# Post-norm decoder layer on one core: up and down units in one line through all visits, and pairs that join every four visits

## The chip, the core and the metric

One core of a Trainium2 chip. The metric is the device time of one execution in microseconds. TensorE is called PE, VectorE DVE, ScalarE ACT, GpSimd POOL, SyncE SP; SP issues all DMAs here. A unit is a piece of work named below.

## What is computed

x is 16 sequences of 128 tokens of 256 numbers, float32. Three residual blocks, each followed by a layer norm:

```python
x = layernorm(x + attention(x))            # 16 heads of 16, with biases, output product and bias
x = layernorm(x + recurrence(x, ctx_1024)) # per token and channel, along the tokens:
#   out = A + exp(u + k) * (v * B + max(t - 1, 0))
#   A = exp(-w) * A + (t != 0) * exp(k) * v ;  B = exp(w) * B + (t != 0) * exp(-k)
x = layernorm(x + ffn(x))                  # 8 experts, K = 128 of 128 tokens each:
#   G = softmax(x @ Wg.T); every token goes through every expert:
#   sum over e of G[e] * (gelu(x @ W1[e] + b1[e]) @ W2[e] + b2[e]),  W1[e] 256 x 1024
```

K is as large as the sequence, so the top-k picks every token.

## The kernel before

Sequences go two by two: 8 pairs of 256 tokens. A product of float32 numbers is made of three matmuls on parts (hi x hi, hi x lo, lo x hi), so each operand has a part hi, made on ACT by a copy, and a part lo, made on DVE by `low`, a subtraction (L830).

The FFN is cut into visits. A visit is one expert's turn, expert n % 8 in visit n, for the one or two pairs that are active; a pair joins at visit `JOIN[p]` and stays for 8. With joins (0, 5, 8, 13, 16, 21, 24, 29) there are 37 visits: 0 to 4 and 32 to 36 with one pair, 27 with two. A visit has 8 up units and 8 down units with two pairs, 4 and 4 with one. An up unit (`up`, L627) is 128 or 256 hidden columns: 6 matmuls of 512 columns, or 12 of 256, into one of two `up_ps` banks. ACT makes gelu (`hidden`, L761) into one of three slots of h_all, then the copy h_hi (`hidden_hi`, L754) into one of four; DVE makes h_lo (`hidden_lo`, L997). A down unit (`down`, L649) is 12 matmuls that add into `down_ps`, which holds the visit's output until `add_expert` (L1002) on DVE has added it, times the gate, to acc; the first down unit of the next visit waits for all of that (semaphore `added`, L653).

The order of units is written out by `items(n)` (L57): U0 U1 U2 D0 U3 D1 U4 ... U7 D5 D6 D7 within each visit. Every engine walks the same items, and each item also carries steps of the next pair's attention and recurrence: pair p has 64 steps laid over `LENGTH[p]` items from item `BEGIN[p]`. Per item the order on ACT is: h_hi of the unit before if that was an up unit (L809), gelu of this one (L811), the attention steps, splits. DVE has add_expert at item 0, h_lo, the steps, splits. The steps named in the prediction: maxima of the scores (8, 10, 24, 26), exp (12, 13, 28, 29), transposes of the probabilities and their copies pt_hi and pt_lo (14, 17, 30, 32), product with the values (16, 19, 31, 34), exps of the recurrence (44), scans and the mix (48 to 52), transposes back (54), transposes to x2t, which the pair's FFN needs (58), routing (60 to 62), gates (0 and 3 of the next pair's steps). Exp and gelu are in different ACT tables, so changing between them is an ACT_TABLE_LOAD; copies need none.

Weights: visits 0 to 7 load float32 pieces (`load_piece`), split them on ACT and DVE and write both parts to DRAM (`keep`); visits 8 to 31 read those parts back (`load_kept`); visits 32 on load and split again. There are 4 pieces for each of w1 and w2. The tables SPLIT and LOAD say at which item a piece is brought in, once the last unit that reads its slot is past. A finished pair is normalised (`finish`) and stored by SP at items 2 and 4 of the next visit.

Of the kernel before, what the change touches and what calls it, by code (L numbers as in the profile page):

```python
# [20 lines left out]
def decoder_layer(nc, x, ctx_in, wq, wk, wv, wo, cols, bv, bo, wg, w1, b1, w2, b2, out):  # L21
# [31 lines left out]
    def units(n):  # L53

        return FC if len(active(n)) == 2 else G

    def items(n):  # L57

        m = units(n)
        order = [("U", u) for u in range(LAG)]  # L60
        for u in range(LAG, m):
            order += [("D", u - LAG), ("U", u)]
        return order + [("D", u) for u in range(m - LAG, m)]

    def splits(n, k):

        table = SPLIT_TWO if len(active(n)) == 2 else SPLIT_ONE
        return [(n + d, i, q) for d, i, q in table.get(k, []) if n + d < VISITS and n + d not in KEPT]

    def loads(n, k):  # L70

        table = LOAD_TWO if len(active(n)) == 2 else LOAD_ONE
        return [(n + d, i, q) for d, i, q in table.get(k, []) if n + d in KEPT]

    FIRST_UNIT = list(itertools.accumulate((units(n) for n in range(VISITS)), initial=0))
    FIRST_ITEM = list(itertools.accumulate((len(items(n)) for n in range(VISITS)), initial=0))
# [11 lines left out]
    with ExitStack() as ctx:  # L88
# [122 lines left out]

        def sequence(n, i, q):

            return 2 * G * turn_of(n) + ORDER.index((i, q))

        def by_chunk(t):
            return t.rearrange("p (c n) -> p c n", c=C)
# [136 lines left out]
        def _(sp):  # L354
# [7 lines left out]
                sp.dma_start(ctx_sb[:], ctx_in[PAIR * p:PAIR * (p + 1)].rearrange("j s d -> s j d")).then_inc(ctx_loaded, 16)  # L362

            def load_piece(m):
                n, j = divmod(m, 2 * G)
                if n >= E:
                    n += len(KEPT)
                if n >= VISITS:
                    return
                i, q = ORDER[j]  # L370
                if m >= RAW:
                    before, was = divmod(m - RAW, 2 * G)
                    which, part = ORDER[was]
                    sp.wait_ge((w1_ready, w2_ready)[which], G * before + part + 1)
# [39 lines left out]
                load_piece(m)  # L414
            load_x(1)
            load_ctx(1)
            for m in range(2 * G - 1):
                load_piece(m + RAW)
            for m in range(2 * G - 1):
                keep(0, *ORDER[m])  # L420

            for n in range(VISITS):
                for k in range(len(items(n))):
# [12 lines left out]
                    if k == STORE_ITEM:  # L436
                        for p in range(NPAIR):
                            if n == JOIN[p] + E:
                                store(p)
            store(NPAIR - 1)  # L440
            sp.wait_ge(stored, 16 * NPAIR)

# [2 lines left out]
        def _(pe):  # L445
# [203 lines left out]
            def down(n, u):  # L649

                unit = FIRST_UNIT[n] + u
                if u == 0 and n > 0:
                    pe.wait_ge(added, EVACUATED[n])  # L653
                weights(n, 1, u * G // units(n))
                pe.wait_ge(h_ready, unit + 1)
                pairs = len(active(n))
                for k in range(2 // pairs):
                    c = u if pairs == 2 else 2 * u + k
                    for a in range(pairs):
                        for j in range(PAIR):  # L660
# [12 lines left out]
                if s in ROUTE_STEP:  # L673
                    route(0, ROUTE_STEP.index(s))
            for n in range(VISITS):
                for k, (kind, u) in enumerate(items(n)):
                    if kind == "U":
                        up(n, u)
                    else:
                        down(n, u)  # L680
                    if n == 0:
                        for part in FIRST_ROUTE.get(k, []):
                            route(0, part)
# [10 lines left out]
        def _(act):  # L694
# [108 lines left out]
                if s in ROUTE_STEP:  # L803
                    route(0, ROUTE_STEP.index(s))
            for n in range(VISITS):
                order = items(n)
                for k, (kind, u) in enumerate(order):
                    if k > 0 and order[k - 1][0] == "U":
                        hidden_hi(n, order[k - 1][1])  # L809
                    if kind == "U":  # L810
                        hidden(n, u)  # L811
                    if n == 0:
                        for part in FIRST_ROUTE.get(k, []):
                            route(0, part)
# [12 lines left out]
        def _(dve):  # L827
# [240 lines left out]
                if s in ROUTE_STEP:  # L1068
                    route(0, ROUTE_STEP.index(s))
            for n in range(VISITS):  # L1070
                order = items(n)
                left = [p for p in range(NPAIR) if n == JOIN[p] + E]
                for k, (kind, u) in enumerate(order):
# [4 lines left out]
                    if k > 0 and order[k - 1][0] == "U":  # L1078
                        hidden_lo(n, order[k - 1][1])
                    if n == 0:  # L1080
                        for part in FIRST_ROUTE.get(k, []):
                            route(0, part)
# [9 lines left out]
                    if k == NORM3_ITEM:  # L1092
                        for p in left:
                            finish(p, 1)
            add_expert(VISITS - 1)
# [5 lines left out]
        def _(pool):  # L1101
# [61 lines left out]
                for i, q in FIRST_SPLIT.get(s, []):  # L1163
                    split_lo(0, i, q)
            for n in range(VISITS):
                for k in range(len(items(n))):
                    if k == 0:
                        for p in range(NPAIR):
                            if n == JOIN[p] + E:
                                finish(p)  # L1170
# [25 lines left out]
ORDER = [(0, 0), (0, 1), (1, 0), (0, 2), (1, 1), (0, 3), (1, 2), (1, 3)]  # L1196
SPLIT_TWO = {1: [(0, 1, 3)], 3: [(1, 0, 0)], 6: [(1, 0, 1)], 8: [(1, 1, 0)], 10: [(1, 0, 2)], 12: [(1, 1, 1)],
             14: [(1, 0, 3)], 15: [(1, 1, 2)]}
LOAD_TWO = {0: [(0, 1, 3)], 2: [(1, 0, 0)], 5: [(1, 0, 1), (1, 1, 0)], 9: [(1, 0, 2), (1, 1, 1)], 13: [(1, 0, 3), (1, 1, 2)]}
LOAD_ONE = {0: [(0, 1, 3)], 1: [(1, 0, 0)], 2: [(1, 0, 1)], 3: [(1, 0, 2), (1, 1, 0)], 5: [(1, 0, 3), (1, 1, 1)], 6: [(1, 1, 2)]}  # L1200
SPLIT_ONE = {1: [(0, 1, 3)], 2: [(1, 0, 0)], 3: [(1, 0, 1)], 4: [(1, 1, 0)], 5: [(1, 0, 2)], 6: [(1, 1, 1), (1, 0, 3)],
             7: [(1, 1, 2)]}
# [39 lines left out]
```

## Time and profile before

| | before |
|---|---|
| median of 3 runs | 1026.37 us (1025.46 to 1026.95) |
| the profiled execution | 1025.53 us, its span 1023.8 |
| PE busy | 917.6 us, 90% |
| DVE busy | 602.8 us, 59% |
| ACT busy | 602.0 us, 59% |
| DMA | 170.33 MB, mean 166 GB/s |

The profile gives for each engine when it was busy, and for each idle time the instruction that ended it. Matmul ends are modelled, and consecutive matmuls overlap in the records, so the time of one is the distance of two starts. The granted clock is a share of 2.4 GHz; 0.5 is the lower level, 1.2 GHz.

### The profile page before, as it was taken

The numbers are of one execution on the slowest core, as the hardware profiler recorded it, in microseconds if no ns is written. First come the engines' busy times: TensorE is split into PE (matmuls) and PEld (weight loads), VectorE is DVE, ScalarE is ACT, GpSimd is POOL, SyncE is SP. The second block draws the span as 40 slices with busy tenths as digits, with TensorE's granted clock in tenths as the row PEclk, the third lists the DMA queues.
The fourth block names the chain that finished last, engine by engine and source line by source line (L and its number), as shares of the span: only waits on it lengthen the run. The fifth ranks groups of instructions, "written<-read, shape, count | busy, mean of one in ns | idle before, by whom it ended". The sixth has DMA issues, their size and how long they took to land.

```text
span 1023.8 us, 17885 instructions
## 1 busy us (share of the span) xinstructions
PE 917.6 (90%) x6672; PEld 824.0 (80%) x6672; DVE 602.8 (59%) x1254; ACT 602.0 (59%) x1017; POOL 84.2 (8%) x116
## 2 busy tenths in 40 slices
PE   4558697988799989999899989999899989999997
PEld 3457586778688879888788879888798888899997
DVE  6747667776565555565556645565556636333765
ACT  4437775666556655555556655555566645444685
POOL 3301001100020001100020001100011000000000
PEclk8667987999999999999999999999999999999999
DMA  6337879755554545454544455445454545565350
GB/s 208 102 126 258 278 251 316 255 198 179 172 168 142 157 140 173 128 173 135 160 150 150 139 167 156 150 149 158 134 167 128 164 141 158 175 195 155 118 171 11
DMA packets 143541, 170.33 MB, mean 166 GB/s; under 512 B 11080, under 2 KB 110688, under 8 KB 143456
## 3 DMA queue, kind: packets, MB, share of 16 engines
q1 hardware_dynamic: 143456, 169.19, 52.3%
q8 instruction: 54, 0.88, 0.4%
q14 instruction: 31, 0.25, 0.1%
HBM read 133.50 MB, written 35.65 MB: 165 GB/s over the span
## 4 chain that ended last, share of the span: by engine, by line
PE 72%; DVE 12%; ACT 11%; issue 3%; DMA 0%; POOL 0%; SPq 0%; POOLq 0%; ACTq 0%; DVEq 0%
PE up_ps L448 11%; PE up_ps L450 10%; PE up_ps L449 10%; PE down_ps L664 10%; PE down_ps L666 9%; PE down_ps L665 9%; ACT probs L717 2%; ACT L717 2%; DVE h_lo L830 2%; DVE pt_lo L905 2%; PE bank L487 2%; PE bank L448 2%; PE bank L470 1%; PE bank L450 1%; PE bank L449 1%
## 5 line engine op out<-in xcount | busy, mean ns | idle before, releaser
L768 ACT ACTIVATE h_all<-up_ps,b_all 128x512 f32<-128x512 f32 (+1 forms) x296 | 182.4, 631 | 344.3 <-PE up_ps L450 340.0
L664 PE MATMUL down_ps<-w_hi,h_hi 128*128 128x256 f32 x1024 | 300.6, 294 | 32.0 <-DVE h_lo L830 31.9
L665 PE MATMUL down_ps<-w_lo,h_hi 128*128 128x256 f32 x1024 | 292.3, 285 | 0.0
L666 PE MATMUL down_ps<-w_hi,h_lo 128*128 128x256 f32 x1024 | 292.3, 285 | 0.0
L830 DVE TENSOR_TENSOR h_lo<-h_all,h_hi 128x512 fp32r<-128x512 f32 x256 | 176.7, 692 | 191.8 <-ACT h_hi L759 190.7
L664 PEld LDWEIGHTS down_ps<-w_hi,h_hi 128*128 128x128 f32 x1024 | 198.0, 193 | 46.2 <-issue 32.4
L448 PE MATMUL up_ps<-x2t_hi,w_hi 128*128 128x512 f32 (+1 forms) x592 | 224.7, 380 | 0.9 <-DVE x2t_lo L830 0.9
L449 PE MATMUL up_ps<-x2t_lo,w_hi 128*128 128x512 f32 (+1 forms) x592 | 219.4, 371 | 0.0
L450 PE MATMUL up_ps<-x2t_hi,w_lo 128*128 128x512 f32 (+1 forms) x592 | 219.3, 370 | 0.0
L665 PEld LDWEIGHTS down_ps<-w_lo,h_hi 128*128 128x128 f32 x1024 | 198.6, 194 | 4.4
L666 PEld LDWEIGHTS down_ps<-w_hi,h_lo 128*128 128x128 f32 x1024 | 198.6, 194 | 0.0
L759 ACT ACTIVATE h_hi<-h_all 128x512 fp32r<-128x512 f32 x256 | 161.8, 632 | 5.2
L450 PEld LDWEIGHTS up_ps<-x2t_hi,w_lo 128*128 128x128 f32 x592 | 115.0, 194 | 19.0
L448 PEld LDWEIGHTS up_ps<-x2t_hi,w_hi 128*128 128x128 f32 x592 | 116.0, 196 | 13.3 <-DVE x2t_lo L830 1.3
L449 PEld LDWEIGHTS up_ps<-x2t_lo,w_hi 128*128 128x128 f32 x592 | 116.1, 196 | 10.6
L830 DVE TENSOR_TENSOR w_lo<-w_raw,w_hi 128x512 fp32r<-128x512 f32 x97 | 66.0, 701 | 37.4 <-ACT w_hi L781 37.4
L1105 POOL TENSOR_TENSOR var_eps<-moments,eps_row 128x2 f32<-128x2 f32 x24 | 10.1, 422 | 790.8 <-DVE moments L841 790.8
L781 ACT ACTIVATE w_hi<-w_raw 128x512 fp32r<-128x512 f32 x104 | 62.7, 629 | 1.1 <-issue 1.1
L1010 DVE SCALAR_TENSOR_TENSOR acc<-down_ps,gate,acc 128x256 f32<-128x256 f32 x112 | 47.0, 476 | 27.5 <-PE down_ps L666 27.5
L905 DVE TENSOR_TENSOR pt_lo<-bank,pt_hi 128x512 f16<-128x512 f32 x58 | 37.4, 686 | 32.1 <-ACT pt_hi L724 32.1
L890 DVE TENSOR_REDUCE neg_max<-bank 128x4 f32<-128x512 f32 x62 | 39.8, 684 | 20.4 <-PE bank L487 20.1
L717 ACT ACTIVATE probs<-probs 128x512 f32<-128x512 f32 x64 | 36.7, 620 | 8.7 <-DVE probs L897 8.5
(172 smaller groups left out, 1008.5 us busy)
## 6 DMA issues: line engine op xcount, KB each, us to landing
w_hi<-w_parts SPq DMA_DIRECT2D x192, 256.0 KB, 3.1
w_lo<-w_parts SPq DMA_DIRECT2D x192, 256.0 KB, 3.4
w_raw<-in_w_dram SPq DMA_DIRECT2D x104, 256.0 KB, 3.8
w_parts<-w_hi SPq DMA_DIRECT2D x64, 256.0 KB, 3.7
w_parts<-w_lo SPq DMA_DIRECT2D x64, 256.0 KB, 4.1
x_in<-in_x_dram SPq DMA_DIRECT2D x8, 256.0 KB, 3.8
ctx_sb<-in_ctx_dram SPq DMA_DIRECT2D x8, 256.0 KB, 4.3
out_dram<-acc SPq DMA_DIRECT2D x8, 256.0 KB, 2.4
```

Source lines behind the costliest of these rows:

```text
L448: nc.tensor.matmul(ps, hi, rhs_hi, start=first, stop=False)
L449: nc.tensor.matmul(ps, hi, rhs_lo, start=False, stop=False)
L450: return nc.tensor.matmul(ps, lo, rhs_hi, start=False, stop=last)
L664: nc.tensor.matmul(ps, hi, w2h[:, c, :], start=c == 0 and j == 0, stop=False, skip_group_check=True)
L665: nc.tensor.matmul(ps, hi, w2l[:, c, :], start=False, stop=False, skip_group_check=True)
L666: mm = nc.tensor.matmul(ps, lo, w2h[:, c, :], start=False, stop=c == FC - 1 and j == PAIR - 1, skip_group_check=True)
L717: nc.scalar.activation(probs[:, u % 2, i], probs[:, u % 2, i], ACT.Exp).then_inc(probs_ready, 1)
L759: nc.scalar.activation(h_hi[:, unit % HALF, :], h_all[:, unit % HALL, :], ACT.Copy).then_inc(h_hi_ready, 1)
L768: a = nc.scalar.activation(h_all[:, unit % HALL, k * wide:(k + 1) * wide], up_ps[unit % 2][:, k * wide:(k + 1) * wide], ACT.Gelu_apprx_tan ...
L781: nc.scalar.activation(piece((w1_hi, w2_hi)[i], i, q), raw(m, i), ACT.Copy)\
L830: return nc.vector.tensor_tensor(dst, src, hi.bitcast(F32), ALU.subtract)
L905: nc.vector.tensor_tensor(pt_lo[:, u % 2, i], by_head(turned(p, u)[i]), pt_hi[:, u % 2, i], ALU.subtract)\
```

## The change

One line of units runs through all visits: `plan()` lists all up units in order and puts a down unit behind the up unit that is three later (for the first down unit of a visit four later). A two-pair visit is then U0 D5' U1 D6' U2 D7' U3 U4 D0 D1 U5 D2 U6 D3 U7 D4, where ' is the visit before. A pair joins every four visits (0, 4, 8, ... 28), which makes 36 visits, 28 of them with two pairs. The second pair's steps are laid over the first 28 items, visits 0 to 3; the third's over visits 4 to 7; from visit 8 on the steps begin with a visit, as before. A down unit waits for each `down_ps` bank by itself. add_expert, finish and store follow the last down unit of a visit by 1, 3 and 5 items. The tables of splits and loads are written anew for the new line, and the order of the pieces follows them.

```diff
-    def items(n):
-        m = units(n)
-        order = [("U", u) for u in range(LAG)]
-        for u in range(LAG, m):
-            order += [("D", u - LAG), ("U", u)]
-        return order + [("D", u) for u in range(m - LAG, m)]
+    def plan():
+        ups = [(n, u) for n in range(VISITS) for u in range(units(n))]
+        lines, downs = [[] for _ in range(VISITS)], 0
+        for g, (n, u) in enumerate(ups):
+            lines[n].append(("U", n, u))
+            while downs + LAG + (ups[downs][1] == 0) <= g:
+                lines[n].append(("D",) + ups[downs])
+                downs += 1
+        return lines[:-1] + [lines[-1] + [("D",) + unit for unit in ups[downs:]]]
...
+    def up_before(i):
+        return [LINE[i - 1][1:]] if i > 0 and LINE[i - 1][0] == "U" else []
+
+    def ended(i):
+        return [(n, [p for p in range(NPAIR) if n == JOIN[p] + E - 1]) for n in range(VISITS - 1) if LAST_DOWN[n] == i]
...
             def down(n, u):
                 unit = FIRST_UNIT[n] + u
-                if u == 0 and n > 0:
-                    pe.wait_ge(added, EVACUATED[n])
...
                     for a in range(pairs):
+                        if c == 0 and n > 0 and a < len(active(n - 1)):
+                            pe.wait_ge(added, EVACUATED[n - 1] + PAIR * (a + 1))
...
-                for k, (kind, u) in enumerate(order):
-                    if k > 0 and order[k - 1][0] == "U":
-                        hidden_hi(n, order[k - 1][1])
+                for k, (kind, visit, u) in enumerate(ITEMS[n]):
+                    for unit in up_before(FIRST_ITEM[n] + k):
+                        hidden_hi(*unit)
                     if kind == "U":
-                        hidden(n, u)
+                        hidden(visit, u)
...
-                    if k == 0 and n > 0:
-                        add_expert(n - 1)
+                    for done, left in ended(FIRST_ITEM[n] + k - 1):
+                        add_expert(done)
                         for p in left:
                             finish(p, 0)
...
-JOIN = (0, 5, 8, 13, 16, 21, 24, 29)
-BEGIN = (None, 0, 40, 88, 152, 216, 280, 344, 408)
-LENGTH = (None, 40, 48, 64, 64, 64, 64, 64, 64)
+JOIN = (0, 4, 8, 12, 16, 20, 24, 28)
+BEGIN = (None, 0, 28, 93, 157, 221, 285, 349, 413)
+LENGTH = (None, 28, 64, 64, 64, 64, 64, 64, 64)
...
-NORM3_ITEM, STORE_ITEM = 2, 4
+NORM3_AFTER, STORE_AFTER = 3, 5
+FIRST_PIECES = [(0, 0, 0), (0, 0, 1), (0, 0, 2), (0, 0, 3), (0, 1, 0), (0, 1, 1), (0, 1, 2)]
+FREE_FIRST = {0: [(0, 1, 3)], 1: [(1, 0, 0)], 2: [(1, 0, 1)], 3: [(1, 0, 2)]}
...
+        [{1: [(1, 0, 0)], 2: [(0, 1, 2)], 3: [(1, 0, 1)], 5: [(1, 0, 2)], 6: [(0, 1, 3)]},
+         {2: [(0, 1, 2)], 3: [(1, 0, 0)], 6: [(0, 1, 3)], 7: [(1, 0, 1)], 10: [(1, 1, 0)], 11: [(1, 0, 2)], 14: [(1, 1, 1)],
+          15: [(1, 0, 3)]}]]
```

## Rows read from the trace of the kernel before

**Rows 1.** Stretches: busy us (x instructions) of PE, PEld, DVE, ACT, POOL; clock, DMA
```profile
64.20:179.90 115.70, 92.58 (x716) 88.42 (x717) 78.38 (x162) 82.34 (x151) 8.85 (x10) 0.84 0.75 246
179.90:284.60 104.70, 90.01 (x663) 78.98 (x662) 69.57 (x141) 66.94 (x111) 7.41 (x8) 0.98 0.61 202
518.40:634.80 116.40, 110.56 (x807) 97.91 (x806) 67.00 (x142) 67.56 (x108) 11.04 (x14) 1.00 0.49 152
959.40:1005.80 46.40, 46.36 (x386) 45.66 (x385) 35.23 (x64) 37.97 (x80) 1.24 (x2) 1.00 0.44 137
```

**Rows 2.** Waits of PE, 518.4 to 634.8: us in total, times, longest us
```profile
PE down_ps L664 <- DVE h_lo L830: 5.7, 4, 2.9
```

**Rows 3.** Waits of PE over the whole span
```profile
PE down_ps L664 <- DVE h_lo L830: 31.9, 23, 3.9
```

**Rows 4.** Timeline of PE: start, us, first matmul of an up, a down, an up unit
```profile
615.99 0.39 PE L448 MATMUL up_ps<-x2t_hi,w_hi 128*128 128x512 f32 x1
...
617.38 0.28 PE L664 MATMUL down_ps<-w_hi,h_hi 128*128 128x256 f32 x1
...
618.82 0.39 PE L448 MATMUL up_ps<-x2t_hi,w_hi 128*128 128x512 f32 x1
```

**Rows 5.** Timeline of PE: pair 0's first and last transposes, pair 1's last
```profile
3.88 1.09 PE L470 MATMUL bank<-ident,x_in 128*128 128x128 f32 x4 [3.88 <-DMA x_in<-in_x_dram]
...
62.13 1.11 PE L585 MATMUL bank<-ident,x 128*128 128x128 f32 x4 [3.27 <-DVE x L848]
...
174.26 0.66 PE L585 MATMUL bank<-ident,x 128*128 128x128 f32 x4 [0.27 <-DVE x L848]
```

**Rows 6.** Timeline of ACT at the end of visit 17
```profile
571.93 0.69 ACT L768 ACTIVATE h_all<-up_ps,b_all 128x512 f32<-128x512 f32 x1 [2.23 <-PE up_ps L450]
572.64 1.28 ACT L717 ACT_TABLE_LOAD   x1
573.93 1.16 ACT L717 ACTIVATE probs<-probs 128x512 f32<-128x512 f32 x2
...
576.55 1.06 ACT L724 ACTIVATE pt_hi<-bank 128x512 f16<-128x512 f32 x2
```

**Rows 7.** Timeline of PE: the first up unit behind that product with the values
```profile
578.71 0.48 PE L448 MATMUL up_ps<-x2t_hi,w_hi 128*128 128x512 f32 x1
```

**Rows 8.** Timeline of DVE at the end of visit 17
```profile
577.15 1.29 DVE L905 TENSOR_TENSOR pt_lo<-bank,pt_hi 128x512 f16<-128x512 f32 x2 [0.83 <-ACT pt_hi L724]
```

**Rows 9.** Timeline of DVE: step 24, in visit 17
```profile
565.34 1.29 DVE L890 TENSOR_REDUCE neg_max<-bank 128x4 f32<-128x512 f32 x2 [1.30 <-PE bank L487]
566.54 1.28 DVE L897 TENSOR_TENSOR probs<-bank,neg_max 128x512 f32<-128x512 f32 x2
```

**Rows 10.** Timeline of DVE: first and last of six small operations for the gates
```profile
516.31 0.17 DVE L980 TENSOR_REDUCE route_sum<-route_exps 128x2 f32<-128x16 f32 x1 [0.32 <-ACT route_exps L749]
...
517.21 0.17 DVE L830 TENSOR_TENSOR gate_all<-gate,gate_all 128x16 fp32r<-128x16 f32 x1
```

**Rows 11.** Timeline of ACT at the end of visit 18
```profile
601.45 0.69 ACT L768 ACTIVATE h_all<-up_ps,b_all 128x512 f32<-128x512 f32 x1 [1.91 <-PE up_ps L450]
...
605.60 0.66 ACT L759 ACTIVATE h_hi<-h_all 128x512 fp32r<-128x512 f32 x1
606.28 1.28 ACT L768 ACT_TABLE_LOAD   x1
```

**Rows 12.** Timeline of DVE at the start of visit 19
```profile
608.84 1.66 DVE L1010 SCALAR_TENSOR_TENSOR acc<-down_ps,gate,acc 128x256 f32<-128x256 f32 x4 [1.86 <-PE down_ps L666]
610.42 1.36 DVE L863 TENSOR_TENSOR_SCAN inc_b<-decay_row,inc_b 128x128 f32<-128x128 f32 x4
...
613.67 1.27 DVE L830 TENSOR_TENSOR h_lo<-h_all,h_hi 128x512 fp32r<-128x512 f32 x2
...
618.18 0.69 DVE L955 TENSOR_TENSOR exp_k<-exp_k,y1t 128x512 f32<-128x512 f32 x1
```

**Rows 13.** Timeline of PE: the transposes of the mix, visit 19
```profile
620.21 0.38 PE L577 MATMUL bank<-ident,exp_k 128*128 128x128 f32 x2
```

More of the change, by code:

```diff
@@ L55, in units, with table @@
         return FC if len(active(n)) == 2 else G
-    def items(n):
-        m = units(n)
-        order = [("U", u) for u in range(LAG)]
-        for u in range(LAG, m):
-            order += [("D", u - LAG), ("U", u)]
-        return order + [("D", u) for u in range(m - LAG, m)]
+    def plan():
[7 more added lines that the diff above has]
+        return lines[:-1] + [lines[-1] + [("D",) + unit for unit in ups[downs:]]]
+    ITEMS = plan()
+    LINE = [item for line in ITEMS for item in line]
+    LAST_DOWN = [max(i for i, (kind, m, _) in enumerate(LINE) if kind == "D" and m == n) for n in range(VISITS)]
+    def table(n):
+        if n == 0:
+            return FREE_FIRST
+        return FREE[len(active(n - 1)) - 1][len(active(n)) - 1]
     def splits(n, k):
-        table = SPLIT_TWO if len(active(n)) == 2 else SPLIT_ONE
-        return [(n + d, i, q) for d, i, q in table.get(k, []) if n + d < VISITS and n + d not in KEPT]
+        return [(n + d, i, q) for d, i, q in table(n).get(k, []) if n + d < VISITS and n + d not in KEPT]
     def loads(n, k):
-        table = LOAD_TWO if len(active(n)) == 2 else LOAD_ONE
-        return [(n + d, i, q) for d, i, q in table.get(k, []) if n + d in KEPT]
+        return [(n + d, i, q) for d, i, q in table(n).get(k, []) if n + d in KEPT]
+    def up_before(i):
+        return [LINE[i - 1][1:]] if i > 0 and LINE[i - 1][0] == "U" else []
+    def ended(i):
+        return [(n, [p for p in range(NPAIR) if n == JOIN[p] + E - 1]) for n in range(VISITS - 1) if LAST_DOWN[n] == i]
     FIRST_UNIT = list(itertools.accumulate((units(n) for n in range(VISITS)), initial=0))
-    FIRST_ITEM = list(itertools.accumulate((len(items(n)) for n in range(VISITS)), initial=0))
+    FIRST_ITEM = list(itertools.accumulate((len(line) for line in ITEMS), initial=0))
+    PIECES = FIRST_PIECES + [piece for n in range(VISITS) for k in range(len(ITEMS[n])) for piece in splits(n, k)]
     EVACUATED = list(itertools.accumulate((PAIR * len(active(n)) for n in range(VISITS)), initial=0))
@@ L212, in sequence @@
         def sequence(n, i, q):
-            return 2 * G * turn_of(n) + ORDER.index((i, q))
+            return PIECES.index((n, i, q))
         def by_chunk(t):
@@ L364, in load_piece @@
             def load_piece(m):
[L365 to L368, printed above, removed]
+                if m >= len(PIECES):
                     return
-                i, q = ORDER[j]
+                n, i, q = PIECES[m]
                 if m >= RAW:
-                    before, was = divmod(m - RAW, 2 * G)
-                    which, part = ORDER[was]
-                    sp.wait_ge((w1_ready, w2_ready)[which], G * before + part + 1)
+                    before, which, part = PIECES[m - RAW]
+                    sp.wait_ge((w1_ready, w2_ready)[which], G * turn_of(before) + part + 1)
                 if i == 0:
@@ L416, in _ @@
             load_ctx(1)
-            for m in range(2 * G - 1):
+            for m in range(len(FIRST_PIECES)):
                 load_piece(m + RAW)
-            for m in range(2 * G - 1):
-                keep(0, *ORDER[m])
+            for first_piece in FIRST_PIECES:
+                keep(*first_piece)
             for n in range(VISITS):
-                for k in range(len(items(n))):
+                for k in range(len(ITEMS[n])):
                     for visit, i, q in splits(n, k):
@@ L435, in _ @@
                             load_ctx(p + 1)
[L436 to L439, printed above, removed]
+                    for _, left in ended(FIRST_ITEM[n] + k - STORE_AFTER):
+                        for p in left:
+                            store(p)
             store(NPAIR - 1)
@@ L675, in _ @@
             for n in range(VISITS):
-                for k, (kind, u) in enumerate(items(n)):
+                for k, (kind, visit, u) in enumerate(ITEMS[n]):
                     if kind == "U":
-                        up(n, u)
+                        up(visit, u)
                     else:
[L680 to L683, printed above, removed]
+                        down(visit, u)
+                    for part in FIRST_ROUTE.get(FIRST_ITEM[n] + k, []):
+                        route(0, part)
                     for p, s in steps(FIRST_ITEM[n] + k):
@@ L805, in _ @@
             for n in range(VISITS):
-                order = items(n)
-                for k, (kind, u) in enumerate(order):
-                    if k > 0 and order[k - 1][0] == "U":
-                        hidden_hi(n, order[k - 1][1])
+                for k, (kind, visit, u) in enumerate(ITEMS[n]):
+                    for unit in up_before(FIRST_ITEM[n] + k):
+                        hidden_hi(*unit)
                     if kind == "U":
-                        hidden(n, u)
-                    if n == 0:
-                        for part in FIRST_ROUTE.get(k, []):
-                            route(0, part)
+                        hidden(visit, u)
+                    for part in FIRST_ROUTE.get(FIRST_ITEM[n] + k, []):
+                        route(0, part)
                     for p, s in steps(FIRST_ITEM[n] + k):
@@ L1070, in _ @@
             for n in range(VISITS):
-                order = items(n)
-                left = [p for p in range(NPAIR) if n == JOIN[p] + E]
-                for k, (kind, u) in enumerate(order):
-                    if k == 0 and n > 0:
-                        add_expert(n - 1)
+                for k in range(len(ITEMS[n])):
+                    for done, left in ended(FIRST_ITEM[n] + k - 1):
+                        add_expert(done)
                         for p in left:
                             finish(p, 0)
[L1078 to L1082, printed above, removed]
+                    for unit in up_before(FIRST_ITEM[n] + k):
+                        hidden_lo(*unit)
+                    for part in FIRST_ROUTE.get(FIRST_ITEM[n] + k, []):
+                        route(0, part)
                     for p, s in steps(FIRST_ITEM[n] + k):
@@ L1091, in _ @@
                         split_lo(visit, i, q)
-                    if k == NORM3_ITEM:
+                    for _, left in ended(FIRST_ITEM[n] + k - NORM3_AFTER):
                         for p in left:
@@ L1165, in _ @@
             for n in range(VISITS):
[L1166 to L1170, printed above, removed]
+                for k in range(len(ITEMS[n])):
+                    for _, left in ended(FIRST_ITEM[n] + k - 1):
+                        for p in left:
+                            finish(p)
                     for p, s in steps(FIRST_ITEM[n] + k):
```

8 lines of the change are left out of this document (1 added, 7 removed), and 3 rows, old and new, of the table FREE.

## The prediction

> **What bounds the kernel now.** Read the stretches first [rows 1]. From visit 8 to visit 27 the kernel repeats one pattern of four visits, in which the next pair's attention is fitted; one of its five turns stands there (518.4 to 634.8, 116.4 us). TensorE is busy 110.6 us of it, VectorE and ScalarE 67 to 68 us. So PE is the bound, and it loses 5.8 us a turn. Who ends that loss [rows 2]: down units that wait for h_lo, four waits, 5.7 us. Over the span the same wait is the largest kind, 31.9 us [rows 3]. Visits 0 to 4 are different (first line of [rows 1]): 115.7 us with PE busy 92.6 at a granted clock of 0.84 and DMA at 0.75; visits 5 to 7 take 104.7 us with 90.0 busy.
>
> PE's own work follows from its issue times [rows 4]: an up unit takes 1.39 us (615.99 to 617.38), a down unit 1.44 us (to 618.82). A visit with two pairs is 8 of each, 22.6 us; with one pair 4 units of each, twelve 256-column matmuls in each, so 4 x 2 x 1.44 = 11.5 us; the last stretch of [rows 1] has four such visits in 46.4, 11.6 each. Attention of one pair on PE is 110.6 - 4 x 22.6 = 20 us.
>
> **Part 1: 37 visits become 36.** Ten one-pair visits and 27 two-pair visits become 8 and 28: the same 64 visits by a pair. PE's columns are the same, and 2 x 11.6 - 22.6 = 0.6 us is all that this saves. One visit's splitting of weights goes (8 pieces on ScalarE and VectorE, 2 MB read), at the end where PE is busy 46.36 of 46.40 us: nothing. So the count of visits is worth under 1 us; the change lives by the waits.
>
> **Part 2: visits 0 to 3.** Until the start of visit 4 PE now has 16 up and 12 down units (28 x 1.44 = 40.5 us) and pair 1's attention (20 us). What ends the stretch is pair 1's chain, because visit 4 needs its x2t. Before, its last transposes for that are at 174.26, 110 us after 64.2, behind 36 of 40 items [rows 5]. The bounds: if each item costs the chain nothing, it stays at 110 us; if all of the items' share is on it, take pair 0, whose chain ran without FFN units from its first transposes at 3.9 us to the same point at 62.1 [rows 5]: 58 us, with the projections' loads and splits in it, for which I take off 5: 53. Then 36 items cost 110 - 53 = 57 us, 1.6 each, and the 25 items that are left cost 40: 93 us. With three more items and the routing matmuls visit 4 starts at 64.2 + 97 us. I take the 97: with VectorE 78 and ScalarE 82 of 115.7 us busy [rows 1], each step stands in a queue behind the units' and splits' work, so items count; the bound on the other side is 110. DMA moves 28 pieces x 768 KB = 22 MB, 227 GB/s over 97 us, under the 246 of that stretch before.
>
> **Part 3: visits 4 to 7.** Four two-pair visits (90.5), the four downs of visit 3 (5.8) less the three of visit 7 that come later (4.3), attention 20: 112. Idle before in visits 5 to 7: 14.7. Now attention has four visits, but the splits of this stretch are in the queues; 5.8 (a turn now) and 15 are the bounds; I take 11.5, nearer to the upper, for 8 splits a visit on both elementwise engines. Sum 123.5. Visits 0 to 7 therefore take 97 + 123.5 = 220.5 against 220.4 before. At the end the last four visits carry three more down units: 46.4 + 4.3 = 50.7 against 57.0 for five. Together -6.2 us; + 0.3 for the last visit, where the added wait stands behind one up unit only.
>
> **Part 4: the line, in each turn.** What goes: the last down unit of a visit no longer stands two downs behind its up unit. New order within a visit: U0 D5 U1 D6 U2 D7 U3 U4 D0 D1 U5 D2 U6 D3 U7 D4 (D5 to D7 of the visit before). All waits of [rows 2] are at these ends, so 5.7 us a turn go. What is late next, place by place, with attention's steps at their item numbers:
>
> (a) Softmax to values, second half (steps 28 to 31 at items 12 to 15). Before, item 12 is U7: ScalarE does gelu, table load, exps, the copy h_hi, exps, and pt_hi begins 4.62 us after the gelu did (571.93 to 576.55) [rows 6]; the values are done when the next up begins at 578.71, 6.78 after that gelu [rows 7], with only 0.2 waited for pt_lo. Now item 12 is U6 and U7 is item 14, just ahead of the copies pt_hi: a table load (1.28) and a gelu (0.69) stand between exp and pt_hi. pt_hi begins 2.0 to 2.1 us later, and nothing covers it: PE has D3, U7, the transposes and D4, about 5.1 us, and then waits to 8.2 for the first pt_lo, which now begins 0.6 after pt_hi and takes 0.65 [rows 8]. +2.1 us.
>
> (b) The same for the first half (steps 12 to 16): a further up unit stands before the values, so the loss is between 2.1 - 1.4 = 0.7 and 2.1; I take 1.0.
>
> (c) Scores (steps 8, 10 and 24, 26). Step 8 mod 16 is now at D0. ScalarE's copy h_hi of U4 needs the slot that D0 frees, and VectorE takes h_lo of U4 before the maxima: 0.85 + 0.75 = 1.6 us after D0 (0.63 and 0.69 are their own times), then neg_max and probs 2.5 [rows 9] = 4.1; PE reaches the next scores after 0.5 + 1.44 + 1.39 = 3.35. +0.75 twice, 1.5. Bounds 0 and 2.5 each.
>
> (d) Gates: exp of the logits (step 62, item 14) now comes behind U7's gelu: 0.2 + 0.7 + 1.28 + 0.2 + 1.1 of small VectorE operations (516.31 to 517.38) [rows 10] = 3.5 after U7, while PE is back after D4 and U0 in 2.8. +0.7.
>
> (e) Recurrence (steps 44 to 54). Before: gelu at 601.45, h_hi at 605.60, then the table load to 607.56 [rows 11]; VectorE's scans wait for the evacuation and run from 610.42, units' h_lo follow at 613.67, the mix is ready at 618.87 [rows 12], PE's transposes come at 620.21 [rows 13], 18.76 after the gelu. Now: the same up to the table load's end (6.1), gelu, h_hi, h_lo of U7 to 8.2, scans 3.25, then the 5.2 from 613.67 less one h_lo of 0.7: 15.95. PE gets there after five ups and five downs, 14.0, and waits 2.0. Transposes at 16.0 instead of 18.76: -2.75. The waits for h_lo near here (the longest 2.9 [rows 2]) are gone, but 2.0 came in their place.
>
> (f) down waits for `added` bank by bank. D7 is followed by U3 and U4, 2.8 us; four additions take 1.66 [rows 12], two of them 0.9. Queued behind that wait on PE are all later units, on ScalarE the copy of U4. By hand VectorE has them done 0.4 to 1 us in time. Nothing; if late, up to 1 us a visit.
>
> Sum: 2.1 + 1.0 + 1.5 + 0.7 - 2.75 = +2.55 us a turn, idle 8.4 instead of 5.8. Five turns: +12.7. SP's queue: the loads of kept weights keep 13 items or more between a slot's last reader and its next use, about 20 us, and the store has moved behind item 10; nothing. Visits 28 to 31 have no attention and no idle: 0.
>
> **A rule weighed.** A table load here is 1.28 us, and the exps start 0.01 us behind it (572.64 to 573.93) [rows 6]. The Trainium skill (ScalarE: Activation LUTs, "What ACT_TABLE_LOAD costs") says that each switch also costs a drain of about 1.38 us, 2.66 in all. It speaks against this change: the load that now stands ahead of pt_hi would cost more. By the row the sum stands; by the page (a) and (b) would each be an estimated 1.4 us worse. The trace disagrees; by that rule 1047 us.
>
> **How the numbers follow.** -6.2 + 0.3 + 12.7 = +6.8 on a span of 1023.8: 1030.6. The profiled execution was 1025.53, 1.7 over its span; the median of the three runs is 1026.37, 0.8 over that. So 1033 us. A measurement of this kernel can tell about 0.2% (2 us) from no change.
>
> - Forecast, 1033 (own range 1024 to 1042): 0.50. The lower 0.10 of it counts as no change.
> - Faster: downs no longer wait, and nothing takes the place. It decides where pt_hi isn't behind U7's gelu in time (the table load running early, or VectorE never late): the idle of a turn falls to 2 us, 5 x 6.4 = 32 less: 1001. For it: 31.9 us are one kind of wait [rows 3], all of it touched. Against: attention's chains [rows 6, 11, 12] are as long as PE's work beside them. 0.20.
> - A turn keeps its 116.3 us, gains and losses even: 1026.4 - 6 = 1020.5. 0.12, of which 0.02 within no change.
> - Pair 1's chain doesn't shorten (a bound of part 2): visit 4 starts 13 us later, 1046. For it: busy queues, DMA at 0.75, half-rate clock when PE waits. 0.15.
> - The page's drain: 1047, 0.03.
>
> Faster 0.20 + 0.10 = 0.30, no change 0.12, slower 0.58. The range leaves out the lower half of the second case and what lies over the fourth: 1006 to 1048.
>
> **What would show it.** Right: the waits of down units for h_lo nearly gone; waits of the values for pt_lo about 3 us in every second visit of a turn and 2 in every first; scores waiting for probs 0.7 ten times; transposes of the mix waiting 2 us once a turn; a turn of 119 us; visit 4 starting at 161 us. Wrong: a turn under 116 us with pt_hi straight behind exp; downs waiting for acc; visit 4 at 175 us. The forecast fails most easily in (a) and (c), which count five times, and in part 2.

## The result, and the profile after

The changed kernel takes 1048.36 us (median of 4 runs, 1046.83 to 1051.85), before 1026.53: the ratio is 1.0219, 95% interval 1.0192 to 1.0246. The forecast was 1033 us, a ratio of 1.007, with a range of 1006 to 1048. Two of the ten executions of turn_first below were slow ones (1480 and 2223 us); its ratio is of the other eight, whose median is 1025.1 us.

The page of the changed kernel, its span and PE's line, then the same view of stretches as [rows 1]: visits 0 to 3, visits 4 to 7, one turn (the pattern of four visits, here 16 to 19), all five turns (visits 8 to 27), and the last visits up to their last unit.

```profile
span 1047.3 us, 17753 instructions
...
PE 922.9 (88%) x6624; PEld 826.1 (79%) x6624; DVE 599.4 (57%) x1246; ACT 595.8 (57%) x1001; POOL 85.8 (8%) x116
...
65.60:162.90 97.30, 70.67 (x572) 66.86 (x573) 66.95 (x137) 61.49 (x117) 8.55 (x10) 0.85 0.63 207
162.90:297.40 134.50, 117.60 (x818) 104.66 (x817) 85.61 (x172) 89.83 (x146) 8.89 (x10) 0.95 0.65 212
536.30:655.90 119.60, 112.14 (x806) 98.95 (x806) 66.82 (x142) 67.37 (x109) 9.57 (x12) 0.99 0.47 148
297.40:896.90 599.50, 562.69 (x4023) 497.11 (x4022) 333.29 (x704) 335.99 (x540) 46.20 (x58) 0.98 0.47 147
989.00:1039.50 50.50, 49.66 (x415) 49.16 (x414) 34.15 (x62) 36.39 (x76) 1.57 (x2) 1.00 0.30 90
```

Against [rows 1] a turn is 3.2 us longer, and visits 4 to 7 take 134.5 us. PE's waits over the whole span; the same two largest kinds in the kernel before; and those of the turn:

```profile
PE bank L539 <- DVE pt_lo L920: 38.3, 28, 4.7
PE bank L595 <- DVE exp_k L970: 31.6, 8, 11.2
PE bank L505 <- DVE probs L912: 11.8, 15, 2.3
PE bank L621 <- DVE gate_all L845: 5.1, 6, 2.2
...
PE down_ps L682 <- DVE acc L1025: 1.5, 2, 0.8
```

```profile
PE bank L577 <- DVE exp_k L955: 16.4, 3, 8.1
PE bank L521 <- DVE pt_lo L905: 15.0, 16, 4.9
```

```profile
PE bank L539 <- DVE pt_lo L920: 4.3, 3, 2.8
PE bank L595 <- DVE exp_k L970: 1.8, 1, 1.8
PE bank L505 <- DVE probs L912: 0.7, 2, 0.3
PE bank L621 <- DVE gate_all L845: 0.6, 1, 0.6
```

The 31.9 us of down units waiting for h_lo are gone without a rest. In their place stand waits of attention's matmuls: for pt_lo (23 us more over the span), for the mix (exp_k, 15 more), for probs and for the gates (4 more each, from 7.5 and 1.1).

### The profile page after: what moved, and what is told of

Same layout as the page of the kernel before. It is cut to its first block, busy times and chain, and to the rows that moved or that the text cites. A ratio compares the mean times of both kernels' runs of the same rounds, so it can differ in the third digit from the quotient of the medians.

```text
span 1047.3 us, 17753 instructions
## 1 busy us (share of the span) xinstructions
PE 922.9 (88%) x6624; PEld 826.1 (79%) x6624; DVE 599.4 (57%) x1246; ACT 595.8 (57%) x1001; POOL 85.8 (8%) x116
## 3 DMA queue, kind: packets, MB, share of 16 engines
q1 hardware_dynamic: 141280, 167.10, 50.5%
## 4 chain that ended last, share of the span: by engine, by line
PE 61%; DVE 17%; ACT 15%; issue 6%; POOL 0%; DMA 0%; SPq 0%; ACTq 0%; POOLq 0%; DVEq 0%
PE down_ps L682 9%; PE up_ps L466 8%; PE up_ps L468 8%; PE up_ps L467 8%; PE down_ps L684 8%; PE down_ps L683 8%; ACT L785 2%; DVE pt_lo L920 2%; ACT probs L734 2%; ACT h_hi L776 2%; ACT h_all L785 2%; ACT L734 2%; DVE probs L912 2%; DVE h_lo L845 2%; PE bank L488 1%
## 5 line engine op out<-in xcount | busy, mean ns | idle before, releaser
L468 PE MATMUL up_ps<-x2t_hi,w_lo 128*128 128x512 f32 (+1 forms) x576 | 217.1, 377 | 0.0
L467 PE MATMUL up_ps<-x2t_lo,w_hi 128*128 128x512 f32 (+1 forms) x576 | 216.8, 376 | 0.0
L682 PEld LDWEIGHTS down_ps<-w_hi,h_hi 128*128 128x128 f32 x1024 | 198.0, 193 | 11.2 <-issue 2.4
L468 PEld LDWEIGHTS up_ps<-x2t_hi,w_lo 128*128 128x128 f32 x576 | 111.4, 193 | 19.7
L466 PEld LDWEIGHTS up_ps<-x2t_hi,w_hi 128*128 128x128 f32 x576 | 112.3, 195 | 15.0 <-issue 1.3
L467 PEld LDWEIGHTS up_ps<-x2t_lo,w_hi 128*128 128x128 f32 x576 | 112.7, 196 | 10.6
L845 DVE TENSOR_TENSOR w_lo<-w_raw,w_hi 128x512 fp32r<-128x512 f32 x89 | 62.2, 700 | 49.1 <-ACT w_hi L798 49.0
L798 ACT ACTIVATE w_hi<-w_raw 128x512 fp32r<-128x512 f32 x96 | 59.7, 629 | 0.0
L539 PE MATMUL bank<-v_cat,pt_hi 128*128 128x51 bf16 x256 | 21.6, 192 | 39.6 <-DVE pt_lo L920 38.3
L539 PEld LDWEIGHTS bank<-v_cat,pt_hi 128*128 128x128 f16 x256 | 16.5, 101 | 48.2 <-issue 40.7
```

What stands on the lines that cost most here:

```text
L466: nc.tensor.matmul(ps, hi, rhs_hi, start=first, stop=False)
L467: nc.tensor.matmul(ps, hi, rhs_lo, start=False, stop=False)
L468: return nc.tensor.matmul(ps, lo, rhs_hi, start=False, stop=last)
L798: nc.scalar.activation(piece((w1_hi, w2_hi)[i], i, q), raw(m, i), ACT.Copy)\
L845: return nc.vector.tensor_tensor(dst, src, hi.bitcast(F32), ALU.subtract)
```

## The experiments

The times stand first. Every ratio is to the kernel before, run on the same chip, where its median was 1026.0 to 1027.1 us.

| kernel | us | ratio (95%) |
|---|---|---|
| the change | 1048.36 | 1.0219 (1.0192 to 1.0246) |
| joins_only | 1009.21 | 0.9836 (0.9821 to 0.9850) |
| line_only | 1040.29 | 1.0141 (1.0126 to 1.0156) |
| turn_first | 1025.39 | 0.9984 (0.9969 to 0.9999) |
| pair2_aligned | 1040.85 | 1.0140 (1.0125 to 1.0156) |
| score_first | 1044.31 | 1.0179 (1.0158 to 1.0201) |
| rec_early | 1044.27 | 1.0176 (1.0153 to 1.0199) |
| turn_rec | 1011.25 | 0.9850 (0.9830 to 0.9871) |
| old_front | 1032.63 | 1.0058 (1.0041 to 1.0076) |
| all_fixes | 984.66 | 0.9592 (0.9576 to 0.9609) |
| old_front_all | 973.67 | 0.9497 (0.9478 to 0.9516) |
| joins_fixed | 988.91 | 0.9619 (0.9591 to 0.9646) |

### Each half of the change alone: joins_only and line_only

```diff
 (the kernel before)
-JOIN = (0, 5, 8, 13, 16, 21, 24, 29)
-BEGIN = (None, 0, 40, 88, 152, 216, 280, 344, 408)
-LENGTH = (None, 40, 48, 64, 64, 64, 64, 64, 64)
+JOIN = (0, 4, 8, 12, 16, 20, 24, 28)
+BEGIN = (None, 0, 32, 96, 160, 224, 288, 352, 416)
+LENGTH = (None, 32, 64, 64, 64, 64, 64, 64, 64)
```

> The kernel before, with its order of units within each visit, and only the joins of the change: a pair every four visits, 36 visits, the second pair's steps over the 32 items of visits 0 to 3 and the third's over visits 4 to 7. Theory (the joins are worth little by themselves, the new line costs): turns of 116.4 us as before, visits 0 to 3 100 to 106 us, in all 1015 to 1025 us. Rival (the earlier join costs, since the second pair's attention and then the third's have fewer visits to hide in while weights are split): 1035 us or more with turns of 116.4.

The other half is the changed kernel with the joins of before (`BEGIN` 0, 36, 85, 149, ...).

> The changed kernel with the joins of before (0, 5, 8, 13, 16, 21, 24, 29), 37 visits, the second pair's steps over the 36 items of visits 0 to 4, the third's over the 49 items of visits 5 to 7. Theory (the new line costs 3.3 us in each of the five turns, the joins little): turns of 119.6 us, in all 1040 to 1050 us. Rival (the joins cost): at most 1032 us.

Stretches of joins_only (visits 0 to 3, 4 to 7, 16 to 19), then of line_only (visits 0 to 4, 16 to 19):

```profile
64.10:157.20 93.10, 77.16 (x620) 72.74 (x621) 69.94 (x143) 67.42 (x127) 8.83 (x10) 0.86 0.74 242
157.20:276.70 119.50, 113.12 (x807) 99.94 (x806) 80.63 (x166) 80.34 (x135) 7.21 (x8) 0.97 0.68 227
511.50:628.10 116.60, 112.00 (x806) 99.03 (x805) 67.04 (x142) 67.61 (x108) 9.64 (x12) 0.99 0.49 152
```

```profile
64.60:170.00 105.40, 80.23 (x668) 75.04 (x669) 75.62 (x151) 75.33 (x141) 8.81 (x10) 0.91 0.76 248
...
516.60:636.40 119.80, 112.29 (x806) 99.07 (x805) 66.83 (x142) 67.60 (x109) 9.58 (x12) 0.99 0.49 148
```

The joins gain 17 us; my expectation was 1 to 11, and it missed because visits 0 to 3 came down to 93.1 us with all their down units, below the 100 to 106 expected. The line alone costs 14 us, turns of 119.8 as expected; in its visits 0 to 4 it even gains (105.4 us and 5.8 for the down units left over, against 115.7 before). On top of the new joins it costs 39 us, and the stretches say where. Five turns are 599.5 us against 586.2 (276.7 to 862.9 in joins_only), so 13. Visits 0 to 3 are 97.3 us plus four downs left over (5.8) against 93.1, so 10. Visits 4 to 7 are 134.5, less the 5.8 they inherit, plus the 4.3 they hand on, against 119.5, so 13.5. The rest, about 3, lies ahead of visit 0 and behind visit 27.

### What stands between exp and pt_hi: turn_first

ScalarE of the changed kernel at the end of visit 17, to be read beside [rows 6]; then VectorE and PE there, beside [rows 7, 8]:

```profile
592.35 0.69 ACT L785 ACTIVATE h_all<-up_ps,b_all 128x512 f32<-128x512 f32 x1 [2.62 <-PE up_ps L468]
593.06 1.28 ACT L734 ACT_TABLE_LOAD   x1
594.35 1.16 ACT L734 ACTIVATE probs<-probs 128x512 f32<-128x512 f32 x2
...
595.93 1.14 ACT L734 ACTIVATE probs<-probs 128x512 f32<-128x512 f32 x2
597.09 1.28 ACT L785 ACT_TABLE_LOAD   x1
598.38 0.69 ACT L785 ACTIVATE h_all<-up_ps,b_all 128x512 f32<-128x512 f32 x1
598.97 1.07 ACT L741 ACTIVATE pt_hi<-bank 128x512 f16<-128x512 f32 x2
```

```profile
599.59 1.29 DVE L920 TENSOR_TENSOR pt_lo<-bank,pt_hi 128x512 f16<-128x512 f32 x2 [2.84 <-ACT pt_hi L741]
...
600.42 0.18 PE L539 MATMUL bank<-v_cat,pt_hi 128*128 128x51 bf16 x1 [2.79 <-DVE pt_lo L920]
```

pt_hi begins 6.62 us after the gelu (592.35 to 598.97) where it was 4.62 [rows 6], behind the table load and the gelu that the prediction put there. The edit on ScalarE:

```diff
+                    turned_first = [(p, s) for p, s in steps(FIRST_ITEM[n] + k) if p < NPAIR and s in TURN_STEP]
+                    for p, s in turned_first:
+                        attend(p, s)
                     if kind == "U":
                         hidden(visit, u)
```

> The changed kernel, with one edit: where an item has an up unit and a step that copies turned probabilities, ScalarE makes the copies pt_hi first and gelu (with its table load) behind them. Theory (a table load and a gelu stand between exp and pt_hi): the wait of the values' product for pt_lo, 3.06 us in every second visit of a turn and 1.78 in the one after the first, falls by about 2 us each; a turn of four visits goes from 119.6 to about 116 to 117 us, and with visits 4 to 7 the kernel from 1048 to 1030 to 1036 us. Rival (the line of units as such is slow, PE's own order leaves too little work between the transposes and the product whatever ScalarE does first): the turn stays at 119 us and the time within 3 us of 1048.

The turn of turn_first, stretch and waits:

```profile
530.80:645.20 114.40, 110.45 (x806) 97.81 (x805) 66.80 (x142) 67.62 (x109) 9.57 (x12) 1.00 0.49 155
```

```profile
PE bank L539 <- DVE pt_lo L924: 0.9, 2, 0.8
```

The wait for pt_lo falls from 4.3 to 0.9 us a turn, the turn from 119.6 to 114.4, which is 2.0 less than before the change. The kernel gains 23 us, more than the 12 to 18 expected. 3.4 us of the 5.2 a turn are the waits; the rest goes with the clock: 1.00 here, and in the changed kernel 0.95 in visit 18, right behind the long wait (see rec_early). The rival, PE's own order, is out. Visits 4 to 7 gain nothing: they take 137.7 us at a clock of 0.93, and the wait of 4.7 us for pt_lo is still in them. So something else holds it there.

### The third pair's steps one item off: pair2_aligned

ScalarE of the changed kernel in visit 5, where `BEGIN` 28 with 17 items in visit 4 puts each step from visit 5 on one item earlier than a later pair has it:

```profile
228.48 1.15 ACT L734 ACTIVATE probs<-probs 128x512 f32<-128x512 f32 x2
229.53 0.62 ACT L798 ACTIVATE w_hi<-w_raw 128x512 fp32r<-128x512 f32 x1
230.17 1.28 ACT L785 ACT_TABLE_LOAD   x1
231.47 0.69 ACT L785 ACTIVATE h_all<-up_ps,b_all 128x512 f32<-128x512 f32 x1
232.17 1.28 ACT L734 ACT_TABLE_LOAD   x1
233.46 1.15 ACT L734 ACTIVATE probs<-probs 128x512 f32<-128x512 f32 x2
...
235.04 1.06 ACT L741 ACTIVATE pt_hi<-bank 128x512 f16<-128x512 f32 x2
```

A gelu comes between the two pairs of exps, with a table load on each side, and a split ahead of it: 6.56 us from the first exps to pt_hi (228.48 to 235.04), against 4.62 in visit 17 of the same kernel (594.35 to 598.97) and 2.62 in [rows 6] (573.93 to 576.55). PE waits 4.7 us for pt_lo there.

```diff
-BEGIN = (None, 0, 28, 93, 157, 221, 285, 349, 413)
+BEGIN = (None, 0, 29, 93, 157, 221, 285, 349, 413)
```

> The changed kernel with the third pair's steps begun one item later (29 instead of 28), so that in visits 5 to 7 they stand at the items at which the later pairs have them. Theory (in visits 5 and 6 the exps stand at down items, with a gelu and two more table loads and a split between the first exp and pt_hi): the wait of 5.1 us in visit 5 falls to about 3, and visits 4 to 7 from 134.5 to 129 to 131 us, the kernel to about 1044. Rival (the splits in the queues or the DMA traffic of visits 0 to 7 hold this stretch): visits 4 to 7 stay within 1 us of 134.5, and the time at 1048.

Visits 4 to 7:

```profile
163.50:290.00 126.50, 115.63 (x818) 101.79 (x817) 82.79 (x165) 82.63 (x141) 10.16 (x10) 0.97 0.69 225
```

134.5 us become 126.5, below the 129 to 131 expected, and the kernel gains 7.5. So most of what that stretch cost beyond 123.5 us was the one item; the splits and the DMA traffic, which are the same in both, are out as its main cause. PE's idle time falls from 16.9 us (134.5 - 117.6) to 10.9, its busy time from 117.6 to 115.6. The longest wait for pt_lo is 2.8 us now; waits for the gates and for probs in visit 4 also became shorter, and what each of these shifts is worth was not tried by itself.

### Smaller waits alone: score_first and rec_early

```diff
 (score_first, on VectorE, ahead of hidden_lo)
+                    scores_first = [(p, s) for p, s in steps(FIRST_ITEM[n] + k) if 1 < p < NPAIR and s in SCORE_STEP]
+                    for p, s in scores_first:
+                        attend(p, s)
 (rec_early)
-REC_STEP = [48, 50, 51, 52]
+REC_STEP = [46, 50, 51, 52]
```

> The changed kernel, with one edit on VectorE: from the third pair on, at an item with scores, their maxima and probs come ahead of the h_lo of the unit before. Theory (the second scores of a half wait because h_lo of U4, which waits through h_hi for D0, is queued ahead of the maxima): the waits of 0.73 us for probs, two in each turn, go; a turn loses 1.4 us, the kernel 7 to 9 us of 1048. Rival (the chain scores, maxima, probs, scores is itself longer than the two units between): the waits stay at 0.5 us or more and the time within 3 us of 1048.

> The changed kernel, with the scans' step at 46 instead of 48, so that VectorE runs them ahead of h_lo of U7 and not behind it. Theory (the transposes of the mix wait for VectorE's queue behind U7's gelu, h_hi and h_lo): the wait of 2.2 us in each turn goes to 0 and the wait of 3.7 in visit 7 to about 1.5; the kernel gains 12 to 16 us. Rival (the chain from the exps through scans to the mix is what lasts, wherever it starts in the queue): the wait stays at 1.5 to 2.2 us and the time within 4 us of 1048.

Both gave 4 us by their medians, which is little more than their spread: the intervals of the ratios (up to 1.0201 and 1.0199) touch that of the changed kernel (from 1.0192). Both did remove their wait: the turn of score_first (533.3 to 652.4, 119.1 us) shows none for probs, that of rec_early none for the mix. In score_first the wait was smaller than the expectation had it: visits 16 and 17 are 31.5 and 32.6 us instead of 31.9 and 33.0, 0.8 a turn and not 1.4, so 4 us in five turns. In rec_early the wait of 1.8 is gone, and yet the turn (536.2 to 655.6) is 119.4 us, 0.2 less than in the changed kernel. Visits 17 and 18 of the changed kernel, then visit 17 of rec_early:

```profile
568.20:601.20 33.00, 28.24 (x233) 24.27 (x232) 17.88 (x33) 20.05 (x31) 0.00 (x0) 0.99 0.46 141
601.20:629.30 28.10, 28.10 (x198) 25.30 (x196) 12.11 (x28) 13.78 (x23) 1.24 (x2) 0.95 0.44 139
```

```profile
568.10:602.70 34.60, 29.80 (x235) 25.84 (x233) 17.94 (x33) 20.20 (x31) 0.00 (x0) 0.95 0.42 135
```

Visit 17 is 1.6 us longer, its clock 0.95 instead of 0.99. A stretch at the lower level (1.2 of 2.4 GHz; the clock is 0.51 from 572.1 to 575.6) follows the wait of 1.4 us for pt_lo at its start. The same wait stands in visit 17 of the changed kernel, and there the clock stays at 1.00 until 600.5, behind the longer wait at the visit's end. The expectation of rec_early failed on this, that of score_first on the size of its wait.

### Does the clock take the gain: turn_rec

turn_first and rec_early together.

> The changed kernel with two edits together: pt_hi ahead of gelu, and the scans' step at 46. Alone the first gave 23 us and the second 4, though it took the wait of 2.2 us out of every turn: visits 9, 13, 17, 21 and 25 became 1.5 us longer, with the granted clock at its lower level for part of them, behind the wait for pt_lo of 1.8 us. Theory (the second edit's gain was lost to the clock that those waits bring down): with that wait gone both show, a turn is 112.3 to 112.6 us, no stretch of a turn at the lower clock, and the kernel at 1008 to 1014 us. Rival (the edit itself lengthens those visits, the scans being earlier in VectorE's queue): visits 9, 13 and so on stay 1.5 us longer than with the first edit alone (29.2 us), a turn is 114 us, the kernel at 1019 us or more.

Visits 16 and 17 of turn_rec:

```profile
523.10:555.00 31.90, 30.98 (x222) 27.14 (x221) 19.93 (x43) 19.47 (x35) 5.39 (x6) 1.00 0.50 154
555.00:584.20 29.20, 27.94 (x235) 24.21 (x233) 17.55 (x32) 18.71 (x29) 0.00 (x0) 1.00 0.52 159
```

Its turn is 112.4 us (523.1 to 635.5), all four visits at full clock; the edit that gave 4 us alone gives 14 on top of turn_first. Visit 17 has the 29.2 us of turn_first, so the scans' place doesn't lengthen it.

### The line in visits 0 to 3: old_front

The order and the splits of before in visits 0 to 3, the second pair's steps over 32 items, the line from visit 4 on, the third pair's steps in visits 5 to 7 as the later pairs have them.

> The changed kernel, with the order of units and the splits of before in visits 0 to 3 (second pair's steps over their 32 items), the line from visit 4 on, and the third pair's steps in visits 5 to 7 at the items of the later pairs. Theory (in the line the second pair's chain has 28 items in place of 32, with the scans and the mix within four, and stands in a wait of 11.4 us): visit 4, with nothing of visit 3 left over, starts at 158 us instead of at 163 with four down units left, and visits 4 to 7 take 122 to 126 us as against 126.5 for the aligned third pair; in all 1030 to 1035 us. Rival (the wait is only shifted): within 4 us of the 1041 that the aligned kernel has.

In the changed kernel, visit 3 holds one long wait of PE, and then the stretches of old_front:

```profile
153.54 1.11 PE L595 MATMUL bank<-ident,exp_k 128*128 128x128 f32 x4 [11.17 <-DVE exp_k L970]
```

```profile
65.10:158.90 93.80, 77.16 (x621) 73.17 (x622) 70.01 (x143) 67.41 (x127) 8.82 (x10) 0.88 0.74 241
158.90:280.00 121.10, 112.34 (x770) 98.76 (x770) 78.69 (x159) 77.54 (x132) 10.06 (x10) 0.94 0.66 215
```

The kernel takes 8 us less than pair2_aligned, within the 1030 to 1035 expected; the wait for the mix is 3.0 us here (at 149.5). In the changed kernel the recurrence's exps, scans and mix stand within items 19 to 22, and PE has nothing to put beside them. Which part of the edit cures it stays open, since it changes the order of units, the splits and the number of items together. The number of items alone doesn't explain it: line_only, with 36 of them, waits 5.9 us for the mix there, joins_only, with 32 in the order of before, 2.9.

### All waits at once: all_fixes, old_front_all, and the order of before cured: joins_fixed

all_fixes has the edits above and on ScalarE the exp of the logits ahead of gelu; old_front_all has them on top of old_front.

> The changed kernel with five edits together: pt_hi ahead of gelu, the exp of the logits ahead of gelu, maxima ahead of h_lo, the scans' step at 46, the third pair's steps one item later. Theory (the waits are separate and each is worth what it is alone): 1048 less 23, 5, 8, 14 and 7.5 us, so 988 to 998 us, a turn of 111 to 113 us with no wait over 1 us. Rival (behind each removed wait another one comes due, as happened with the change itself): 1005 us or more, a turn of 114 us or more.

> The order and splits of before in visits 0 to 3 and the line from visit 4 on, with the four edits to the order within the engines' queues and the third pair's steps at the items of the later pairs. Theory (the line costs in visits 0 to 3, where its wait for the mix is 9 to 11 us, and the edits act as in the kernel with all of them): visit 4 starts at 158 us with nothing left over, 974 to 979 us. Rival (what the front gains is lost in visits 4 to 7): within 2 us of 984.7.

Visits 4 to 7 and a turn of all_fixes, and visits 0 to 3, 4 to 7 and a turn of old_front_all:

```profile
162.50:279.10 116.60, 112.30 (x818) 99.44 (x817) 82.84 (x171) 83.09 (x143) 9.79 (x10) 1.00 0.74 244
500.80:611.70 110.90, 109.97 (x806) 98.00 (x805) 67.01 (x142) 67.75 (x109) 9.37 (x12) 1.00 0.52 159
```

```profile
64.10:159.60 95.50, 77.59 (x620) 73.06 (x621) 70.12 (x143) 67.57 (x127) 8.84 (x10) 0.87 0.72 236
159.60:269.10 109.50, 106.61 (x771) 93.62 (x770) 80.11 (x165) 79.47 (x135) 9.48 (x10) 1.00 0.73 238
490.80:601.70 110.90, 109.97 (x806) 98.00 (x806) 67.05 (x142) 67.78 (x109) 9.39 (x12) 1.00 0.52 160
```

Together the edits give 64 us, where turn_first, pair2_aligned, score_first and rec_early alone give 23 + 7.5 + 4 + 4 = 38.5; the exp of the logits was not run alone. The 984.66 us are better than the 988 to 998 expected. The rival (each removed wait lets another come due) is out: PE idles 0.9 us a turn. old_front_all, 973.67 us (974 to 979 expected), beats both kernels, by 5.0% that of before.

Is the line needed for it? joins_fixed is joins_only with the copy h_hi put between a gelu and exps of the same item on ScalarE, and the scans at 46. Its visits 4 to 7 and a turn stand below its expectation.

> The joins of the change with the order of units of before, and that order's own waits taken away by order within the queues: where a step of exps follows a gelu on ScalarE, the copy h_hi of that unit goes between them, and the scans' step is at 46. Theory (the waits of down units for h_lo at a visit's end came from exps queued ahead of h_hi, so they can be removed without the line): the waits of 0.95 and 3.1 us go, a turn falls from 116.3 to 111 to 113 us and the kernel from 1009 to 980 to 992 us. Rival (a visit's end without up units is too short for the way from up to down in any case, the line is needed): the waits for h_lo stay above 1 us, a turn at 114 us or more, the kernel at 998 us or more.

```profile
160.20:283.00 122.80, 114.92 (x807) 101.91 (x807) 81.12 (x166) 80.69 (x135) 7.21 (x8) 0.96 0.68 221
508.20:620.80 112.60, 110.31 (x807) 97.68 (x806) 67.06 (x142) 67.69 (x108) 9.64 (x12) 1.00 0.51 157
```

A turn of 112.6 us, 1.7 above the 110.9 of old_front_all. The waits for h_lo are 0.6 us a turn (4.5 in joins_only), so in the turns what the line was to remove could be had by order within the queues, without the line. In visits 4 to 7 they are not gone: 6.7 us, the longest 4.1. There old_front_all takes 109.5 us, and 113.8 with the three down units (4.3) that it hands on, against 122.8. The 15 us between these two kernels are not the line's alone: old_front_all also has pt_hi, the exp of the logits and the maxima moved ahead in their queues. No run separates that.

## Why the prediction was right or wrong

Where it was right, it was the reading of queues in the turns. Its parts, by its letters:

- (a) and (b): forecast +2.1 and +1.0; pt_hi came 2.00 us later, the waits for pt_lo were 4.3 us a turn (2.8 and 1.4 the two main ones), and turn_first shows the cause.
- (c) 0.75 twice: there, but smaller. Without them (score_first) a turn is 0.8 us shorter, not 1.5.
- (d) +0.7: a wait on the gates, 0.6 by the profile.
- (e) a wait of 2.0 for the mix: 1.8. VectorE ran the scans behind h_lo of U7, where [rows 12] has them behind the additions:

```profile
632.76 0.69 DVE L845 TENSOR_TENSOR h_lo<-h_all,h_hi 128x512 fp32r<-128x512 f32 x1 [1.97 <-ACT h_hi L776]
633.37 1.36 DVE L878 TENSOR_TENSOR_SCAN inc_b<-decay_row,inc_b 128x128 f32<-128x128 f32 x4
...
641.28 0.66 PE L595 MATMUL bank<-ident,exp_k 128*128 128x128 f32 x4 [1.78 <-DVE exp_k L970]
```

- (f) the waits for acc: 1.5 us in the whole run, nothing, as said.
- Visits 0 to 3: 97 forecast, 97.3 measured, and that was luck. The 97 came from a price of 1.6 us for each item of the second pair's chain. By that price joins_only, with four items more, would take 103 us; it took 93.1, with four more down units done. The changed kernel's 97.3 hold a wait of 11.2 us for the mix that part 2 doesn't name. (28 x 1.44 is 40.3 there and not 40.5; nothing hangs on it.)
- The last visits: 50.7 and 50.5.
- The turns: 12.7 us forecast for five, 599.5 - 583.3 = 16.2 measured. PE's idle time grew by 10.5 (from 26.3 to 36.8), less than forecast. Its busy time grew by 5.7 (from 557.0 to 562.7) for the same units, where the forecast had nothing: that is the clock, 0.98 over the five turns, 0.99 before. The prediction priced waits by their length only.

**The step that failed is part 3.** It put visits 4 to 7 at 123.5 us, 112 of PE's work and 11.5 idle; they took 134.5, 117.6 busy and 16.9 idle. That term was mis-sized by 11 of the 16.7 us by which the profiled span (1047.3) exceeds the forecast one (1030.6). About half of the 11 is each of two things:

- The idle time, 5.4 more, and above the upper bound of 15. Both bounds came from stretches in which the steps stand elsewhere: the items of (a) to (e) were laid out for visits from 8 on, and the step numbers were not laid over visits 4 to 7, where the first visit has 17 items. pair2_aligned shows it: with the steps one item later PE idles 10.9 us, close to the 11.5 taken.
- PE's own work, 5.6 more, priced at full clock. The granted clock was 0.95 here. In all_fixes the same 818 matmuls, at a clock of 1.00, are busy 112.3 us, as forecast; in pair2_aligned, at 0.97, 115.6. So the 3 us that pair2_aligned leaves over 123.5 are the clock.

The remaining difference: 3.5 in the turns; 1.4 in the stretch ahead of visit 0 (65.6 instead of 64.2), which varies between 64.0 (score_first) and 66.3 (joins_fixed) among kernels with the same units there; and 0.6 in visits 28 to 31.

The drain that the Trainium skill (ScalarE: Activation LUTs, "What ACT_TABLE_LOAD costs") adds to each switch was not paid here, and its case did not come: in the changed kernel the gelu follows its table load at once (597.09 + 1.28 to 598.38), and (a) has its size without one. And the faster case stood on a true remark, that all waits for h_lo go. It was false that nothing would take their place, but five small edits bring it about: the case had PE idle 2 us a turn and 1001 us in all, all_fixes has 0.9 and 984.66.

## What to carry to other kernels

When the order of work on the bound engine changes, lay the other engines' queues out again, item by item, and look for what now stands between two steps of a chain; a gelu and its table load moved ahead of a copy cost 5.2 us a turn here, nearly all of the 5.7 us of waits that the new order removed. Do this for each stretch whose layout differs, the first and the odd ones too, since the steady turn was forecast within 1 us on average and the odd stretch missed by 11. A forecast that hits can still have the wrong mechanism, as that for visits 0 to 3 did. Where several short waits lie in a row, judge an edit together with the others: the scans' place gave 4 us alone and 14 beside turn_first.

## What the runs showed of the hardware

The clock makes waits cost more than their length, and not evenly. In rec_early a wait of 1.8 us was removed from a turn, and visit 17, ahead of the place of that wait, went from a granted clock of 0.99 to 0.95 and from 33.0 to 34.6 us; the same edit beside turn_first left all four visits at 1.00. In all_fixes and old_front_all, with PE idle 0.9 us a turn, the turn is at 1.00; so it is in turn_first, with 4.0 us idle a turn and no wait over 1.8. Nor does the length of a wait decide it alone: the turn of before has one of 2.9 us [rows 2] and is at 1.00 [rows 1], while the 2.8 us of the changed kernel are followed by the lower level. In visits 4 to 7 the same 818 matmuls were busy 117.6, 115.6 and 112.3 us at clocks of 0.95 (the changed kernel), 0.97 (pair2_aligned) and 1.00 (all_fixes). What brings the clock down in one turn and not in another, with waits so alike, is not settled by these runs.
